# Attention in units of 32 queries and four key groups, with VectorE turning the probabilities

## The chip, the cores and the metric

The kernel runs on one core of a Trainium2 chip, in one launch. The metric is the device time of the whole program in microseconds, the median of the timed runs; lower is better. PE is TensorE's matmul stream, PEld its weight loads, DVE VectorE, ACT ScalarE, POOL GpSimd, SP the SyncE queue.

## The reference, cut to what matters

The program computes three residual layers in turn. The change touches only the first, a cross attention of 32 batches, 64 queries each, 1601 keys each, 16 heads of 16 channels; its inputs and outputs are fp32. The second layer (a cosine circuit with a small FFN) and the third (routed experts) stay as they are.

```python
# x (32, 64, 256), ctx (32, 1601, 256), H = 16, HD = 16, SCALE = 4.0
q = split_heads(layernorm(x) @ Wq.T + bq)
k = split_heads(ctx @ Wk.T + bk)
v = split_heads(ctx @ Wv.T + bv)
score = einsum('bhqd,bhkd->bhqk', q, k) * SCALE
attn = softmax(score, axis=-1)
x = x + merge(einsum('bhqk,bhkd->bhqd', attn, v)) @ Wp.T + bp
```

## The kernel before

Everything that the change touches is in `attention_and_circuit`, a raw program for each engine with semaphores; there is no scheduler, the order of every engine is written out in its own function `batches`.

One batch `n` has eight pairs of heads `p`, and each pair has one 128-row tile of scores: partition 64*e + t is head 2p+e, query t, and the 1601 keys run along the free dimension. `g = 8n + p` counts the pairs of all batches. A pair goes through these stages:

- `scores` (L952): four matmuls of 402 keys into the four banks of `ps_s`. The operands are fp32r and three parts are stacked on 96 rows (`k_st` holds high, low, high of the keys; `bd` holds high, high, low of the queries, block-diagonal over the two heads), so that one pass gives fp32 quality. `k_st` and `bd` are put together by DMAs: `stack_keys` on SP issues 48 copies of keys a batch (L246), `fill_queries` six of queries.
- `take_scores` (DVE, L636) moves all 1608 columns to `probs` in one instruction, times -4, and takes the minimum of each row into `nmax`.
- `exponentials` (ACT, L459) is one activation over 1601 columns with the row sums in `esum`.
- `turn` (PE, L963) transposes the probabilities in 13 pieces of 128x128 into the two banks of `ps_t`; ACT copies the first twelve out (`copy_tiles`, L453, three copies of 512 columns), DVE the thirteenth (`copy_tail`, L668).
- After four pairs `weigh` (L983) multiplies with the values: 13 key tiles times 4 pairs, each on 32 columns of the array, into `ps_o`. The sums of the rows are inverted, spread, turned on PE (`turn_scale`, L970) and multiplied in by `normalise` (L687 to L690). Every two batches `project_out` (L990) and `residual` make a tile of the first layer's output.

Between these, PE computes the keys and values of the next batch in 15 steps: eight of kind "k" (6 matmuls of 402 columns, from `c_hi`, `c_lo` and `w_hi`, `w_lo`), seven of kind "v" (12 matmuls of 256 columns, the last one 6). The helper `three` has the lines L915 to L917. The table `SLOT_STEPS` says which steps stand with which pair. DVE brings the keys out twice, as high and low part (L654, L656), and copies the values (L661, L663). POOL splits the context of the batch after that into high and low part (`split_ctx`, L355 to L360), from a buffer `raw` that SP fills.

The start of the program normalises x, projects the queries, stores their high and low part to DRAM (`q_scr`), and computes batch 0's keys and values before the first scores. The end of the last batch runs over into the second layer, whose orders are the tables `DVE_ORDER`, `ACT_ORDER`, `PE_ORDER`, `POOL_ORDER`.

## Time and profile before

| | us |
|---|---|
| median of 3 runs | 1943.64 (1942.24 to 1943.75) |
| span of the profiled execution | 1941.7 |
| PE busy | 1876.6 (97%) |
| PEld busy | 1777.8 (92%) |
| DVE busy | 1468.1 (76%) |
| ACT busy | 1136.1 (59%) |
| POOL busy | 652.9 (34%) |

The page gives a span and no other time for the profiled execution; it lies 1.9 us under the median of the timed runs, which also hold what stands around the first and the last instruction. Busy time is the union of the instructions of an engine. A PE instruction's duration contains the way through the array, so PE's throughput is read from the distance between starts. One fp32 matmul of the program is two PE instructions in the trace (the 52 of a `weigh` are 104); an fp32r matmul and an fp32 transpose are one.

### The profile page before, as it was taken

To read this page: it belongs to the slowest core of one execution; us is meant where nothing else is said; L and a number is where in the kernel's file an instruction comes from. 1 tells how busy PE (TensorE), PEld (TensorE's weight loads), DVE (VectorE), ACT (ScalarE), POOL (GpSimd) and SP (SyncE) were. 2 spreads that over 40 slices of the span, in tenths; PEclk is the share of its full clock that TensorE was granted. 3 is DMA by queue.
4 is the path that set the end of the run, shared out by engine and by line. 5 is a ranking of instruction groups with operands and counts; after the bars stand their busy time and mean duration, and the time that the engine had idled before them with its cause. 6 is when DMAs were issued, how large, how long until landed. Compare 5 with 4: busy or idle time off the path is not lost. (4 is left out here: it accounts for less than half of the span.)

```text
span 1941.7 us, 46658 instructions
## 1 busy us (share of the span) xinstructions
PE 1876.6 (97%) x18832; PEld 1777.8 (92%) x18832; DVE 1468.1 (76%) x2796; ACT 1136.1 (59%) x1921; POOL 652.9 (34%) x643
## 2 busy tenths in 40 slices
PE   7899999999999999999999999999879889999998
PEld 5899999999999999999999999999867789999998
DVE  6777778777777777777777778777788567766667
ACT  2465666666566656666665566656765436665552
POOL 3222223322222323222223232223031126888860
PEclk9899999999999999999999999999989799999999
DMA  8666666666666666666666666667510236666633
GB/s 272 170 155 162 156 174 169 164 157 159 161 153 167 170 167 167 157 158 157 159 167 164 170 165 162 156 163 189 149 60 23 76 118 209 225 220 218 229 115 132
DMA packets 146790, 313.85 MB, mean 162 GB/s; under 512 B 57888, under 2 KB 77216, under 8 KB 143120
## 3 DMA queue, kind: packets, MB, share of 16 engines
q1 hardware_dynamic: 140672, 295.03, 56.2%
q0 software_dynamic: 4752, 13.38, 2.3%
q8 instruction: 149, 2.44, 0.5%
q10 hardware_dynamic: 1152, 2.47, 0.5%
q14 instruction: 65, 0.53, 0.1%
HBM read 134.20 MB, written 18.35 MB: 79 GB/s over the span
## 5 line engine op out<-in xcount | busy, mean ns | idle before, releaser
L453 ACT COPY a_pT<-a_pst 128x512 f32<-128x512 f32 x768 | 421.2, 583 | 409.0 <-PE a_pst L963 409.0
L459 ACT ACTIVATE a_probs<-a_probs,a_nmax 128x1601 f32<-128x1601 f32 x256 | 418.8, 1636 | 140.0 <-DVE a_probs L636 139.8
L636 DVE TENSOR_SCALAR_CACHE_REDUCE a_probs<-a_pss 128x1608 f32<-128x1608 f32 x256 | 467.3, 1825 | 12.8 <-PE a_pss L952 12.3
L963 PE MATMUL a_pst<-a_id,a_probs 128*128 128x128 f32 (+1 forms) x3328 | 452.6, 275 | 13.7 <-ACT a_pT L453 11.5
L963 PEld LDWEIGHTS a_pst<-a_id,a_probs 128*128 128x128 f32 (+1 forms) x3328 | 382.8, 141 | 51.1 <-issue 21.0
L355 POOL TENSOR_TENSOR a_tick<-a_tick 128x1 f32<-128x1 f32 x62 | 12.0, 193 | 953.4 <-DMA a_raw<-in_ctxT 892.1
L654 DVE TENSOR_SCALAR a_khi<-a_psk,a_bk 128x402 fp32r<-128x402 f32 x250 | 158.5, 634 | 142.9 <-PE a_psk L917 141.3
L360 POOL TENSOR_TENSOR a_clo<-a_raw,a_chi 128x402 fp32r<-128x402 f32 x240 | 247.0, 1060 | 4.8
L952 PE MATMUL a_pss<-a_kst,a_bd 96*128 96x402 f32 x1024 | 240.7, 357 | 6.4 <-DVE a_v L661 5.6
L915 PE MATMUL a_pso<-a_whi,a_chi 128*128 128x256 f32 (+1 forms) x806 | 241.9, 300 | 0.0
L917 PE MATMUL a_pso<-a_whi,a_clo 128*128 128x256 f32 (+1 forms) x806 | 227.2, 282 | 0.0
L916 PE MATMUL a_pso<-a_wlo,a_chi 128*128 128x256 f32 (+1 forms) x806 | 227.1, 282 | 0.0
L952 PEld LDWEIGHTS a_pss<-a_kst,a_bd 96*128 96x128 f32 x1024 | 184.3, 190 | 20.0 <-issue 12.5
L983 PE MATMUL a_pso<-a_pT,a_v 128*32 128x128 f32 x6656 | 196.9, 275 | 0.0
L1657 PE MATMUL e_psg<-e_xh,e_guh 128*128 128x256 f32 x660 | 189.7, 287 | 5.3 <-DVE e_hl L1403 3.8
L915 PE MATMUL a_psk<-a_chi,a_whi 128*128 128x402 f32 x500 | 194.2, 388 | 0.0
L983 PEld LDWEIGHTS a_pso<-a_pT,a_v 128*32 128x32 f32 x6656 | 179.4, 111 | 12.8 <-issue 12.5
L1658 PE MATMUL e_psg<-e_xl,e_guh 128*128 128x256 f32 x660 | 186.8, 283 | 0.0
L1659 PE MATMUL e_psg<-e_xh,e_gul 128*128 128x256 f32 x660 | 186.6, 283 | 0.0
L916 PE MATMUL a_psk<-a_clo,a_whi 128*128 128x402 f32 x500 | 173.4, 347 | 0.0
L917 PE MATMUL a_psk<-a_chi,a_wlo 128*128 128x402 f32 x500 | 173.3, 347 | 0.0
L656 DVE SCALAR_TENSOR_TENSOR a_klo<-a_psk,a_bk,a_khi 128x402 fp32r<-128x402 f32 x250 | 159.0, 636 | 9.0
(251 smaller groups left out, 3511.7 us busy)
## 6 DMA issues: line engine op xcount, KB each, us to landing
a_kst<-a_khi SPq DMA_DIRECT2D x1008, 100.5 KB, 2.6
a_kst<-a_klo SPq DMA_DIRECT2D x504, 100.5 KB, 2.6
a_raw<-in_ctxT SPq DMA_DIRECT2D x60, 804.0 KB, 5.5
f_gur<-in_wgu SPq DMA_DIRECT2D x24, 1408.0 KB, 6.2
f_dr<-in_wd SPq DMA_DIRECT2D x24, 768.0 KB, 7.2
a_bd<-q_scr SPq DMA_DIRECT2D x192, 32.0 KB, 2.0
e_big<-ys_scr SPq DMA_DIRECT2D x8, 512.0 KB, 6.7
a_pT<-in_ctxT SPq DMA_DIRECT2D x2, 1608.0 KB, 9.3
```

Of the source, the lines that this page charges most:

```text
L360: last = nc.gpsimd.tensor_tensor(out=c_lo[:, s, k, cols], in0=src[:, cols], in1=c_hi[:, s, k, cols].bitcast(F32), op=ALU.subtract)
L453: nc.scalar.copy(pT[:, p % HALF, 4 * i:4 * i + 4, :], ps_t[:, i % 2, :].rearrange("p (t q) -> p t q", q=P)).then_inc(t_copied_act, 1)
L459: nc.scalar.activation(pr, pr, ACT.Exp, bias=nmax[:, b, p:p + 1], scale=-1.0, accum_out=esum[:, b, p:p + 1]).then_inc(probs_ready, 1)
L636: nc.vector.tensor_scalar(probs[:, p % 2, :].rearrange("p (b k) -> p b k", b=QK), ps_s[:, :, 0:KQ], -SCALE, None, ALU.mult, ALU.min, accum ...
L915: nc.tensor.matmul(out, a[0], b[0], start=start, stop=False)
L916: nc.tensor.matmul(out, a[0], b[1], start=False, stop=False)
L917: return nc.tensor.matmul(out, a[1], b[0], start=False, stop=stop)
L952: mm = nc.tensor.matmul(ps_s[:, q, 0:KQ], bd[:, b, p, :], k_st[:, p, q * KQ:(q + 1) * KQ], start=True, stop=True)
L963: mm = nc.tensor.transpose(ps_t[0:r, i % 2, (t % 4) * P:(t % 4 + 1) * P], probs[:, p % 2, t * P:t * P + r], a_id_sb[:])
L983: mm = nc.tensor.matmul(ps_o[32 * j:32 * j + 32, 0:P], v_sb[0:r, b, t, 32 * p:32 * p + 32], pT[0:r, j, t, :], start=(t == 0), stop=(t == K ...
L1657: nc.tensor.matmul(out, a[0], b[0], start=start, stop=False)
L1658: nc.tensor.matmul(out, a[0], b[1], start=False, stop=False)
```

## The change

The attention is cut into other units. A half `h = 2n + m` is one batch and one group `m` of eight heads. It has four units `(e, r)`: `e` is the head within each pair, `r` which 32 of the 64 queries. The keys are four groups of 400, each with the last key appended (`KG` = 401), stored in 13 tiles of 128 in which each group has 32 rows, 1664 columns in all instead of 1608. A unit's scores have partition 32*g + query (g is the key group), and the four banks of `ps_s` hold the four pairs `j`.

- `scores` is now 16 fp32 matmuls with 32 rows and 32 columns of the array each, 401 columns long, straight from `keys` (fp32, one copy) and `q_own` (the queries with the other head's channels set to zero by POOL). The stacks `k_st` and `bd`, their DMAs and the detour of the queries through `q_scr` are gone. The keys come out of PSUM once, on ACT (L484), the values too (L491); DVE copies neither.
- `take_scores` is four instructions of 401 columns, `exponentials` four activations of 401 columns.
- The minimum of a row must be shared by the four key groups, since they are one softmax: for every two units PE turns `nmax` (`turn_max`), DVE takes the minimum over groups (`reduce_max`), PE spreads it (`spread_max`), ACT copies it (`copy_bias`).
- `turn` is one VectorE transpose of 1664 columns in blocks of 32x32, from `probs` (a ring of 5) to `pT` (6 slots). The transposes on PE and the copies out of `ps_t` are gone.
- `weigh` has 52 matmuls a half as before, with the four units' columns as its moving operand. The sums of the rows go through POOL (`less_extra` takes the three surplus copies of the last key out, `spread_sums`) and four small matmuls; `normalise` divides.
- The steps have 416 columns for keys; the last value tile has 128 rows.

PE in the middle of the loop before: a key step, one pair's scores, and the transposes of the pair before (a_khi, a_psk, a_kst are key tiles, a_pst the turned probabilities).

```order
L963 MATMUL a_pst<-a_id,a_probs 65x128
L915 MATMUL a_psk<-a_chi,a_whi 128x402
L916 MATMUL a_psk<-a_clo,a_whi 128x402
L917 MATMUL a_psk<-a_chi,a_wlo 128x402
L915 MATMUL a_psk<-a_chi,a_whi 128x402
L916 MATMUL a_psk<-a_clo,a_whi 128x402
L917 MATMUL a_psk<-a_chi,a_wlo 128x402
L952 MATMUL a_pss<-a_kst,a_bd 128x402 x4
L963 MATMUL a_pst<-a_id,a_probs 128x128 x8
```

PE at the turn of a half in the changed kernel: the end of a value step, the spread minima, the weighting, the sums, and the next unit's scores.

```order
L879 MATMUL a_psk<-a_whi,a_chi 128x256
L880 MATMUL a_psk<-a_wlo,a_chi 128x256
L881 MATMUL a_psk<-a_whi,a_clo 128x256
L934 MATMUL a_psm<-a_id,a_low 32x8 x4
L953 MATMUL a_pso<-a_pT,a_v1 32x128 x52
L957 MATMUL a_pso<-a_sin,a_marks 32x128 x4
L919 MATMUL a_pss<-a_keys,a_qown 32x401 x16
L879 MATMUL a_psl<-a_chi,a_whi 128x416
L880 MATMUL a_psl<-a_clo,a_whi 128x416
```

So the 13 transposes with each pair have left PE, and a unit's scores are 16 small matmuls where a pair's were four. DVE before, one pair and the beginning of the next:

```order
L636 TENSOR_SCALAR a_probs,a_nmax<-a_pss 128x1608
L661 COPY a_v<-a_pso 128x512
L668 COPY a_pT<-a_pst 65x128
L654 TENSOR_SCALAR a_khi<-a_psk,a_bk 128x402
L656 SCALAR_TENSOR_TENSOR a_klo<-a_psk,a_bk,a_khi 128x402
```

and DVE in the changed kernel, from the fourth unit of one half to the second of the next:

```order
L662 TENSOR_SCALAR a_probs,a_nmax<-a_pss 128x401 x4
L677 STREAM_TRANSPOSE a_pT<-a_probs 128x1664
L668 TENSOR_REDUCE a_low<-a_psm 8x32
L662 TENSOR_SCALAR a_probs,a_nmax<-a_pss 128x401 x4
L677 STREAM_TRANSPOSE a_pT<-a_probs 128x1664
L687 RECIPROCAL a_sT<-a_pso 128x128
L691 SCALAR_TENSOR_TENSOR a_op<-a_pso,a_marks,a_sT 128x64 x2
L695 SCALAR_TENSOR_TENSOR a_oT<-a_op,a_bv 128x64
L662 TENSOR_SCALAR a_probs,a_nmax<-a_pss 128x401 x4
```

The three copies from PSUM with each pair have left DVE and one transpose with each unit has come.

The diff, cut to its core:

```diff
         def _(dve):
+            def take_scores(h, i):
...
+                for j in range(HALF):
+                    at_max = HALF * (i % 2) + j
+                    nc.vector.tensor_scalar(probs[:, at % RING, j, 0:KG], ps_s[:, j, 0:KG], -SCALE, None,
+                                            ALU.mult, ALU.min, accum_out=nmax[:, group % 2, at_max:at_max + 1]).then_inc(max_ready, 1)
...
+            def turn(h, i):
...
+                nc.vector.transpose(pT[:, turned_slot(h, i)].rearrange("p j k -> p (j k)"), probs[:, at % RING].rearrange("p j k -> p (j k)")).then_inc(turned, 1)
...
+            def period(h):
+                for i in range(HALF):
+                    if h + 1 < NH:
+                        take_scores(h + 1, i)
+                    if i == 1 and h % 4 == 0 and h > 0:
+                        residual(h // 4 - 1)
+                    if h >= 0:
+                        turn(h, i)
+                    if i == 0 and h > 0:
+                        normalise(h - 1)
+                    if i % 2 == 1 and h + 1 < NH:
+                        reduce_max(2 * (h + 1) + i // 2)
...
         def _(pe):
-                for q in range(QK):
-                    mm = nc.tensor.matmul(ps_s[:, q, 0:KQ], bd[:, b, p, :], k_st[:, p, q * KQ:(q + 1) * KQ], start=True, stop=True)
+                for g in range(QK):
+                    for j in range(HALF):
+                        mm = nc.tensor.matmul(ps_s[32 * g:32 * g + 32, j, 0:KG], q_own[32 * j:32 * j + 32, n % 2, m, e, 32 * r:32 * r + 32],
+                                              keys[32 * j:32 * j + 32, m, g * KG:(g + 1) * KG], start=True, stop=True)
...
+            def period(h):
+                steps = steps_in(h)
+                if h > 0:
+                    weigh(h - 1)
+                if h + 1 < NH:
+                    scores(h + 1, 1)
+                for z in steps[0]:
+                    step(*z)
...
+                if h + 1 < NH:
+                    turn_max(2 * h + 2)
+                    scores(h + 1, 2)
+                for z in steps[1]:
+                    step(*z)
+                if h + 1 < NH:
+                    spread_max(2 * h + 2)
+                    scores(h + 1, 3)
+                for z in steps[2]:
+                    step(*z)
+                if h + 1 < NH:
+                    turn_max(2 * h + 3)
+                if h + 2 < NH:
+                    scores(h + 2, 0)
+                for z in steps[3]:
+                    step(*z)
+                if h + 1 < NH:
+                    spread_max(2 * h + 3)
```

`scores` waits until DVE has taken all four banks of the unit before (`max_ready`), and `take_scores` waits for the scores (`s_filled`). `normalise(h-1)` stands on DVE between the first and the second unit of a period and waits for `weigh(h-1)`, which PE runs at the start of that period. `turn(h, i)` waits for that unit's exponentials, which ACT makes between the copies of the steps' results.

## Rows read from the trace of the kernel before

**Rows 1.** The page's busy times, and a stretch of the loop (busy us, clock).

```profile
PE 1876.6 (97%) x18832; PEld 1777.8 (92%) x18832; DVE 1468.1 (76%) x2796; ACT 1136.1 (59%) x1921; POOL 652.9 (34%) x643
...
600.00:1000.00 400.00, 399.43 (x4368) 381.14 (x4367) 314.68 (x564) 245.83 (x375) 109.69 (x114) 1.00 0.65 163
```

**Rows 2.** The waits: who waited for whom, us, times, longest.

```profile
ACT a_pT L453 <- PE a_pst L963: 409.0, 317, 3.2
DVE a_khi L654 <- PE a_psk L917: 141.3, 186, 0.8
```

**Rows 3.** Timeline of PE (start us, us): first line of one `weigh`, two batches earlier.

```profile
616.67 3.05 PE L983 MATMUL a_pso<-a_pT,a_v 128*32 128x128 f32 x104
```

**Rows 4.** Timeline of all engines around the `weigh` at 702.56.

```profile
700.82 1.83 DVE L636 TENSOR_SCALAR_CACHE_REDUCE a_probs<-a_pss 128x1608 f32<-128x1608 f32 x1
...
702.36 0.27 PE L970 MATMUL a_pst<-a_id,a_sc 128*128 128x128 f32 x1
...
702.56 2.78 PEld L983 LDWEIGHTS a_pso<-a_pT,a_v 128*32 128x32 f32 x104 [0.17 <-issue]
702.56 3.05 PE L983 MATMUL a_pso<-a_pT,a_v 128*32 128x128 f32 x104
702.57 0.09 DVE L636 DVE_READ_ACCUMULATOR a_probs<-a_pss 128x1 f32 x1
...
702.93 1.64 ACT L459 ACTIVATE a_probs<-a_probs,a_nmax 128x1601 f32<-128x1601 f32 x1
...
704.47 0.19 ACT L459 ACTIVATION_READ_ACCUMULATOR a_probs<-a_probs,a_nmax 128x1 f32 x1
...
705.54 1.01 PE L952 MATMUL a_pss<-a_kst,a_bd 96*128 96x402 f32 x4
705.75 0.23 DVE L687 TENSOR_TENSOR a_os<-a_pso,a_sT 128x64 f32<-128x64 f32 x1 [1.49 <-PE a_pso L983]
705.89 0.22 DVE L688 TENSOR_TENSOR a_pso<-a_pso,a_sT 128x64 f32<-128x64 f32 x1
```

**Rows 5.** Timeline of PE: a value step from 707.18 to 708.68.

```profile
707.18 0.36 PE L915 MATMUL a_pso<-a_whi,a_chi 128*128 128x256 f32 x1
...
708.68 0.71 PE L963 MATMUL a_pst<-a_id,a_probs 128*128 128x128 f32 x5
```

**Rows 6.** Timeline of PE: key step, scores, eight transposes, next value step.

```profile
709.15 0.43 PE L915 MATMUL a_psk<-a_chi,a_whi 128*128 128x402 f32 x1
...
710.33 0.91 PE L952 MATMUL a_pss<-a_kst,a_bd 96*128 96x402 f32 x4
711.08 1.04 PE L963 MATMUL a_pst<-a_id,a_probs 128*128 128x128 f32 x8
711.87 0.36 PE L915 MATMUL a_pso<-a_whi,a_chi 128*128 128x256 f32 x1
```

**Rows 7.** Instructions of single lines: ns minimum/median/maximum, first and last start us.

```profile
L915 PE MATMUL a_psk<-a_chi,a_whi x500: 339/387/748, 30.9 to 1385.5; 128*128 128x402 f32 x167
...
L983 PE MATMUL a_pso<-a_pT,a_v x6656: 269/273/423, 80.1 to 1434.1; 128*32 128x128 f32 x180, 65*32 65x128 f32 x16
...
L680 DVE TENSOR_TENSOR a_sc<-a_rinv,a_own x64: 291/294/2237, 77.9 to 1425.5; 128x128 f32<-128x128 f32 x64
```

**Rows 8.** Groups by line and shape: xcount, busy us, mean ns, idle before.

```profile
L1151 PE MATMUL f_psf<-f_w,f_hT 128*128 128x256 f32 x256 | 58.4, 388 | 0.8 <-ACT f_hT L616 0.8
...
L661 DVE COPY a_v<-a_pso 128x512 f32<-128x512 f32 x186 | 128.6, 691 | 43.1 <-PE a_pso L917 42.9
...
L741 DVE TENSOR_SCALAR f_t<-f_u 128x512 f32<-128x512 f32 x8 | 3.3, 417 | 0.0
...
L864 DVE TENSOR_TENSOR_SCAN f_t<-f_c,f_hd 128x512 f32<-128x512 f32 x4 | 4.9, 1217 | 0.0
...
L459 ACT ACTIVATE a_probs<-a_probs,a_nmax 128x1601 f32<-128x1601 f32 x256 | 418.8, 1636 | 140.0 <-DVE a_probs L636 139.8
...
L616 ACT ACTIVATE f_hT<-f_psh,f_b 128x512 f32<-128x512 f32 x16 | 10.2, 684 | 7.9 <-PE f_psh L1141 7.7
...
L360 POOL TENSOR_TENSOR a_clo<-a_raw,a_chi 128x402 fp32r<-128x402 f32 x240 | 247.0, 1060 | 4.8
```

More of the change, by code:

```diff
@@ new lines, in _ @@
+            for h in range(NH - 2):
+                period(h)
+            sp.wait_ge(kv_filled, STEPS * B)
+            for dst, src in ((row[:], rows), (id_sb[:], ident), (b1_sb[:], b1), (w2_sb[:], w2), (wr_sb[:], wr), (rb_sb[:], rb)):
+                sp.dma_start(dst, src).then_inc(loaded, 16)
+            sp.wait_ge(x1_free, 16 * (NT - 1) + 1)
+            sp.dma_start(x_t[:], x[NT - 1]).then_inc(x_loaded, 16)
+            sp.dma_start(x1[:, NT - 2, :], x1_scr[NT - 2]).then_inc(x1_loaded[group_of[-1]], 16)
@@ L546, in _ @@
+            for h in range(-1, NH):
+                period(h)
             act.wait_ge(expo_set, 1)
@@ L814, in _ @@
+            for h in range(-1, NH):
+                period(h)
             ch = Chain(dve, dv)
@@ new lines, in turn_max, with spread_max @@
+            def turn_max(group):
+                pe.wait_ge(max_ready, 2 * HALF * (group + 1))
+                if group > 0:
+                    pe.wait_ge(bias_ready, group)
+                nc.tensor.transpose(ps_m[0:2 * HALF, 0:P], nmax[:, group % 2, :], a_id_sb[:]).then_inc(max_turned, 1)
+            def spread_max(group):
+                pe.wait_ge(max_reduced, group + 1)
+                for g in range(QK):
+                    mm = nc.tensor.matmul(ps_m[32 * g:32 * g + 32, P:P + 2 * HALF], lowest[:, group % 2, :], a_id_sb[0:2 * HALF, 0:2 * HALF], start=True, stop=True)
+                mm.then_inc(max_spread, 1)
@@ L1097, in _, with period @@
[L1097 to L1098 removed]
+            pe.wait_ge(cleared, 3)
+            for s in range(FIRST_STEPS):
+                step(0, s)
+            scores(0, 0)
+            def period(h):
+                steps = steps_in(h)
+                if h > 0:
+                    weigh(h - 1)
[3 more added lines that the diff above has]
+                    step(*z)
+                    if h % 4 == 0 and h > 0 and z == steps[0][0]:
+                        project_out(h // 4 - 1)
+                if h % 4 == 0 and h > 0 and not steps[0]:
+                    project_out(h // 4 - 1)
+                if h % 4 == 0 and h > 0:
+                    pe.wait_ge(x1_ready, h // 4)
+                if h + 1 < NH:
[8 more added lines that the diff above has]
+                    step(*z)
+                if h + 1 < NH:
+                    turn_max(2 * h + 3)
[3 more added lines that the diff above has]
+                    step(*z)
+                if h + 1 < NH:
+                    spread_max(2 * h + 3)
@@ L1099, in idle_work @@
+            for h in range(-1, NH):
+                period(h)
             def idle_work(n):
```

762 lines of the change are left out of this document (315 added, 447 removed), and 6 rows, old and new, of tables (ACT_ORDER, DVE_ORDER, PE_ORDER).

## The prediction

> **What bounds the kernel now.** I read the busy times first: PE is busy for 1876.6 of 1941.7 us, and in a stretch of 400 us of the loop for 399.43, at a granted clock of 1.00 (2.4 GHz) [rows 1]. Then the waits: ACT waits 409.0 us for PE's transposes and DVE 141.3 us for PE's key steps [rows 2], while PE waits for nobody. So the loop is as long as PE's stream. One `weigh` starts at 616.67 [rows 3] and the same one two batches on at 702.56 [rows 4]: 42.95 us a batch. The steps begin at 30.9 and the last `weigh` begins its last matmuls at 1434.1 [rows 7]: the stretch that the change touches is 1403 us, the other 539 us stay.
>
> PE's parts are read from start to start. Key step 709.15 to 710.33 = 1.18 us; scores of a pair 710.33 to 711.08 = 0.75; eight transposes 711.08 to 711.87 = 0.79 [rows 6]. Value step 707.18 to 708.68 = 1.50 and five transposes 708.68 to 709.15 = 0.47 [rows 5, 6]. `weigh` with its way in and out 702.36 to 705.54 = 3.18 with one small transpose in it, so about 3.1 [rows 4]. A batch: 8 x (0.75 + 0.79 + 0.47) = 16.1, keys 9.4, values 6 x 1.50 + 0.75 = 9.75, weights 6.2, small things 0.6: 42.1 of the 42.95.
>
> **The change on PE.** It removes the 16.1. Kept: key steps of 416 instead of 402 columns, 8 x 1.22 = 9.8; values 9.8; weights 6.2; output projection 0.25. Added: the sums, eight small instructions each half, 2 x 0.25 = 0.5; `turn_max` and `spread_max`, 4 x 0.24 = 1.0. Without scores this is 27.5 us.
>
> The scores are the term that decides. A unit has 16 fp32 matmuls, 32 instructions in the trace. How long does one occupy its tile? 128 columns last 273 ns [rows 7], 256 columns 388 [rows 8], so 0.90 ns a column: 401 columns take 0.36 us and two instructions one after the other 0.71. No row shows tiles of 32 rows. If all 16 run at once, a unit takes 0.71 plus staggering; if only the four column tiles overlap, 8 x 0.36 = 2.9; if nothing does, 32 x 0.36 = 11.5. The nearest row is `weigh`: 104 instructions of 128 columns in 2.98 us (702.56 to 705.54) are 28.7 ns each, where one alone takes some 0.11, so four column tiles do run at once in fp32, each with its own moving stream from all partitions [rows 4]. The new tiling reads no more streams from a partition than that; new is that four row tiles write into four banks at the same partitions. I take 0.80 and keep 2.9 as the upper end (11.5 would need even the overlap of `weigh` to be lost). 8 x 0.80 = 6.4.
>
> Changing the size of the tiles costs something: before `weigh` PEld is idle 0.17 us by "issue" [rows 4], and the way in and out of `weigh` was about 0.3 us more than its stream. A batch has 8 units of scores, entered and left, and 8 small maxima and spreads: 24 changes by 0.17 = 4.1 us; the bounds are 0 (hidden under the end of the work before) and 24 x 0.25 = 6.0.
>
> The Trainium skill, TensorEngine Tiling (Array Packing), "Key Properties", says that a change of the tiling mode drains the engine; the 0.17 us of [rows 4] agrees in kind. TensorE: Matmul & The Clock Gate, Part 3, reports a packing of 4x4 tiles at 10.6 times the speed of single matmuls; by that, 32 x 0.36 / 10.6 = 1.09 us a unit would be an estimate, 2.3 us a batch over my term. No row here shows it.
>
> PE: 27.5 + 6.4 + 4.1 = **38.0 us a batch**.
>
> **DVE.** It loses the key and value copies and gains the transposes. Taking: 1608 columns last 1.83 us, but the next instruction and the accumulator's read both start 1.75 after the start [rows 4]. The 1207 columns fewer at 1.04 ns (1.83 against 691 ns for 512 columns [rows 4, 8]) leave 0.50 for 401 columns; with the accumulator's 0.09 read apart and no overlap 0.57 + 0.09 = 0.66. I take 0.55, since the read overlapped in the row, with a little for four in a row: 2.2 a unit. Transpose of 1664 columns: no row shows one. Bounds from one-input and scan instructions: 512 columns SBUF to SBUF at 417 ns (about 0.52 ns a column, 1.0 us) and a scan at 1217 ns (about 2.1 a column, 3.6 us) [rows 8]; the taking's rate of 1.04 gives 1.87. I take 1.85, the middle rate, at which most instructions of this engine run. Sum: 8 x (2.2 + 1.85) = 32.4; four `reduce_max` at 0.28 and two `normalise` at about 1.0 (as two of 0.23 and 0.22 and their dependents [rows 4]), the residual's half: 3.8. **36.2 us**.
>
> VectorE (DVE) Microarchitecture Reference, section 3.8, of the Trainium skill says that the transpose front end sustains one element per cycle and lane; by that page it is the middle rate too, and no row here shows it.
>
> **ACT.** It loses three copies of 512 columns a pair, gains the key and value copies, and has four short exponentials for one long. 1601 columns last 1.64 and the accumulator's read starts at 1.54 [rows 4]; against 684 ns at 512 columns [rows 8] that is 0.87 ns a column, so 401 last about 0.59; with the read 0.19 apart 0.78, overlapped as in the row 0.6. I take 0.65: 32 x 0.65 = 20.8, fifteen copies at 0.5 = 7.5, maxima 0.7: **29 us**. POOL keeps its split (8 x 1.06 [rows 8] and the casts) and adds about 16 tiny instructions and two spreads of 512 columns, some 20 us of 38. The 48 + 6 DMAs a batch go; they were beside the path (PE waited for none in the loop) and give nothing.
>
> **How they fit together.** PE 38.0, DVE 36.2, ACT 29: no engine has room to hide another's latency, and they are in lock step. Walk one half, PE's share 19.0. A unit of scores needs the taking of the unit before; the taking needs the scores (0.17 after the last start) and comes after the transpose (1.85). PE has after the scores (0.80 + 0.34) two steps (2.72), 3.9 in all; DVE has 4.05 + 0.28 every second unit. So in the three units without `weigh` DVE is slightly the slower one, and PE waits some tenths before `turn_max` and the scores; in the fourth, `weigh` puts PE 3.4 us ahead of DVE's need, and DVE waits for it at `normalise`, since it only has one taking and one transpose (4.05) before it while PE comes late by up to a step (2.7 + 3.4). Adding the durations along this chain gives 0.6 us of PE waiting a half. **39.3 us a batch.**
>
> The whole: four first steps and a unit, 6; the period that fills the pipe, 21; 62 halves with steps at 19.65, 1218; one half with no steps, bound by DVE (4 x 4.05 + 0.6), 17; the last transposes 9; the last weighting 3.4: 1274, and some 5 less since the last halves overlap. 1270 against 1403 is -133. From the profiled span 1941.7 that is 1808.7, and with the 1.9 that the median lies above it **1811 us**.
>
> **The rivals.**
> 1. *Dearer small instructions.* DVE and ACT at their upper bounds (0.66; 0.78), and transposes held up by POOL: L680, a DVE instruction between two SBUF tensors, has a median of 294 ns and a maximum of 2237 [rows 7]. DVE 8 x (2.64 + 1.95) + 3.8 = 40.5, with waits 42. +2.7 x 31 = +84: 1895.
> 2. *Half the overlap of row tiles*, 1.4 us a unit: +4.8 a batch, less the waits that PE's lateness removes, 42.8 to 43: +3.7 x 31 = +115: 1926. For: no row has it. Against: separate banks.
> 3. *The other side: the DVE transpose at half rate*, 3.6 us. DVE becomes the bound: 8 x (2.2 + 3.6) + 3.8 = 50.2, nothing else late. +10.9 x 31 = +338: 2149. It decides from where DVE's batch passes 43.6, that is a transpose of 2.8 us. For: the data must be filled and drained, in fp32; the scan shows that this engine has instructions at such a rate. Against: most do not.
> 4. *Row tiles do not overlap*, 2.9 us a unit: 54.8 a batch, +15.5 x 31 = +480: 2291.
> 5. *PE's clock falls* to 1.2 GHz in the waits. The stretch of [rows 1] had 1.00 throughout with PE never idle; the new waits are tenths of a microsecond. All of PE's 38 us at half clock would be 76 a batch, a quarter of the loop so would add 300.
>
> **How the numbers follow.** My forecast 0.63, rival 1 0.10, rival 2 0.07, rival 3 0.09, rival 4 0.08, rival 5 0.03. The forecast's own range, with changes of tile size at 0.05 to 0.25 us and takings at 0.50 to 0.60, is 36.8 to 41 us a batch: 1735 to 1865. The range of 8 in 10 takes in rivals 1 and 2: 1735 to 1960. Faster: 0.63 + 0.09 of rival 1 + 0.03 of rival 2 = 0.75. Same (within 0.2%, 4 us, about what a measurement of this kernel can tell): 0.03, from 1 and 2. Slower 0.22.
>
> **What would show it.** In the profile of the changed kernel: a unit's 32 instructions of L919 in about 0.8 us from start to the next step's start (step 1 of the forecast; 1.4 or 2.9 for rivals 2 and 4); L677 at about 1.9 us (3.6 for rival 3); L662 starts 0.55 apart; L465 starts 0.65 apart; successive first lines of L953 19.65 us apart; PE over 90% busy at a clock of 1.00, DVE over 90%. A DVE near 100% with PE waiting for L662 by whole microseconds, or a clock under 1.00 in the loop, would make the prediction wrong; so would a PE busy all the time with scores longer than 1.4 us.

## The result, and the profile after

The changed kernel takes **1827.74 us** (median of 4 runs, 1826.5 to 1828.59) where the kernel before, in runs beside it, took 1942.94 (1941.53 to 1943.75): a ratio of 0.941, 95% interval 0.939 to 0.942. The prediction was 1811 with a range of 1735 to 1960. The profiled execution has a span of 1824.6 us, against the 1808.7 of the sum.

The page's busy times and the same stretch of the loop as in [rows 1]; the columns of the second line are the stretch, PE, PEld, DVE, ACT and POOL busy, the granted clock, the DMA share and GB/s:

```profile
PE 1652.9 (91%) x24272; PEld 1360.0 (75%) x24272; DVE 1566.3 (86%) x3585; ACT 1199.9 (66%) x3297; POOL 892.4 (49%) x1283
```

```profile
600.00:1000.00 400.00, 367.39 (x6607) 284.05 (x6605) 377.12 (x879) 289.13 (x854) 191.82 (x328) 1.00 0.15 48
```

PE was busy for 399.43 of these 400 us and is now for 367.39; DVE was at 314.68 and is now, at 377.12, the busier one. Neither is full. The clock is 1.00 (2.4 GHz) as before. The DMAs' share fell from 0.65 to 0.15; PE had waited for none of them in the loop.

Who waits for whom in 600 to 1000 (us, times, longest), in the place of [rows 2]:

```profile
PEld a_psm L928 <- DVE a_probs L662: 34.3, 36, 1.2
...
PE a_psm L928 <- DVE a_probs L662: 27.0, 36, 1.0
...
DVE a_sT L687 <- PE a_pso L953: 16.0, 10, 1.6
...
PE a_pss L919 <- DVE a_probs L662: 3.0, 5, 0.6
```

(L662 is `take_scores`, here called a taking; L928 is `turn_max`.) The waits have turned round: PE now waits for DVE's takings, ahead of `turn_max`, and DVE for PE's `weigh`. The lines of the loop that cost DVE and PE most (busy us, mean ns of one, idle before):

```profile
L662 DVE TENSOR_SCALAR_CACHE_REDUCE a_probs<-a_pss 128x401 f32<-128x401 f32 x328 | 169.1, 572 | 3.3 <-DVE a_pT L677 3.3
L677 DVE STREAM_TRANSPOSE a_pT<-a_probs 128x1664 f32<-128x1664 f32 x82 | 156.1, 1904 | 0.0
...
L919 PE MATMUL a_pss<-a_keys,a_qown 32*32 32x401 f32 x2592 | 78.1, 507 | 3.0 <-DVE a_probs L662 3.0
...
L687 DVE RECIPROCAL a_sT<-a_pso 128x128 f32<-128x128 f32 x20 | 19.2, 958 | 17.8 <-PE a_pso L953 16.0 <-issue 1.8
L695 DVE SCALAR_TENSOR_TENSOR a_oT<-a_op,a_bv 128x64 f32<-128x64 f32 x20 | 17.8, 892 | 0.7
```

The timeline where one `weigh` ends, a unit of scores runs and the normalisation follows (start us, us; compare [rows 4]):

```profile
607.55 0.40 PE L957 MATMUL a_pso<-a_sin,a_marks 128*32 128x128 f32 x8
...
607.88 0.97 PE L919 MATMUL a_pss<-a_keys,a_qown 32*32 32x401 f32 x32
608.08 0.96 DVE L687 RECIPROCAL a_sT<-a_pso 128x128 f32<-128x128 f32 x1 [0.18 <-issue]
...
608.29 3.12 POOL L313 TENSOR_TENSOR a_clo<-a_raw,a_chi 128x416 fp32r<-128x416 f32 x3
...
608.79 0.46 PE L879 MATMUL a_psk<-a_chi,a_whi 128*128 128x416 f32 x1
...
609.07 0.48 DVE L691 SCALAR_TENSOR_TENSOR a_op<-a_pso,a_marks,a_sT 128x64 f32<-128x64 f32 x2
...
609.58 0.89 DVE L695 SCALAR_TENSOR_TENSOR a_oT<-a_op,a_bv 128x64 f32<-128x64 f32 x1
...
610.39 0.56 DVE L662 TENSOR_SCALAR_CACHE_REDUCE a_probs<-a_pss 128x401 f32<-128x401 f32 x1
```

A unit's 32 instructions hold PE for 0.90 us (607.88 to 608.79). The normalisation holds DVE for 2.31 us (608.08 to 610.39), while POOL subtracts beside it; the taking of the unit whose scores were ready at about 608.9 has to wait for that. The first instructions of successive `weigh` alternate at 18.5 and 20 to 21.4 us; two batches are 78.4 us, **39.2 a batch** against 42.95.

### The profile page after: what moved, and what is told of

Same layout as the page of the kernel before. It is cut to its first block and busy times, and to the rows that moved or that the text cites. A ratio compares the mean times of both kernels' runs of the same rounds, so it can differ in the third digit from the quotient of the medians.

```text
span 1824.6 us, 59184 instructions
## 1 busy us (share of the span) xinstructions
PE 1652.9 (91%) x24272; PEld 1360.0 (75%) x24272; DVE 1566.3 (86%) x3585; ACT 1199.9 (66%) x3297; POOL 892.4 (49%) x1283
## 3 DMA queue, kind: packets, MB, share of 16 engines
q1 hardware_dynamic: 38416, 130.71, 21.4%
## 5 line engine op out<-in xcount | busy, mean ns | idle before, releaser
L465 ACT ACTIVATE a_probs<-a_probs,a_bias 128x401 f32<-128x401 f32 x1024 | 632.2, 625 | 0.0
L662 DVE TENSOR_SCALAR_CACHE_REDUCE a_probs<-a_pss 128x401 f32<-128x401 f32 x1024 | 527.8, 572 | 25.5 <-PE a_pss L919 14.9
L677 DVE STREAM_TRANSPOSE a_pT<-a_probs 128x1664 f32<-128x1664 f32 x256 | 487.3, 1904 | 0.0
L919 PE MATMUL a_pss<-a_keys,a_qown 32*32 32x401 f32 x8192 | 248.0, 509 | 14.2 <-DVE a_probs L662 13.5
L313 POOL TENSOR_TENSOR a_clo<-a_raw,a_chi 128x416 fp32r<-128x416 f32 x240 | 250.2, 1074 | 0.0
L465 ACT ACTIVATION_READ_ACCUMULATOR a_probs<-a_probs,a_bias 128x1 f32 x1024 | 197.2, 193 | 0.0
L484 ACT ACTIVATE a_keys<-a_psk,a_bk 128x401 f32<-128x401 f32 x131 | 77.4, 591 | 96.9 <-PE a_psk L881 96.9
L484 ACT ACTIVATE a_keys<-a_psl,a_bk 128x401 f32<-128x401 f32 x125 | 73.9, 592 | 95.2 <-PE a_psl L881 95.2
L1592 PEld LDWEIGHTS e_psg<-e_xh,e_guh 128*128 128x128 f32 x660 | 125.6, 190 | 6.4 <-issue 6.4
L1593 PEld LDWEIGHTS e_psg<-e_xl,e_guh 128*128 128x128 f32 x660 | 125.7, 191 | 0.0
L1594 PEld LDWEIGHTS e_psg<-e_xh,e_gul 128*128 128x128 f32 x660 | 125.6, 190 | 0.0
L879 PE MATMUL a_psl<-a_whi,a_chi 128*128 128x256 f32 x428 | 123.6, 289 | 0.0
L491 ACT COPY a_v<-a_psl 128x512 f32<-128x512 f32 x99 | 58.0, 586 | 94.9 <-PE a_psl L881 94.9
```

What stands on the lines that cost most here:

```text
L313: last = nc.gpsimd.tensor_tensor(out=c_lo[:, n % 2, k, cols], in0=src[:, cols], in1=c_hi[:, n % 2, k, cols].bitcast(F32), op=ALU.subtract)
L465: nc.scalar.activation(z, z, ACT.Exp, bias=bias[:, group % 4, at_bias:at_bias + 1], scale=-1.0, accum_out=esum[:, h % 2, j, 2 * e + r:2 * ...
L484: nc.scalar.activation(keys[:, m, q * KG:(q + 1) * KG], step_bank(at)[:, 0:KG], ACT.Identity, bias=bk_sb[:, m:m + 1]).then_inc(kv_copied, 1)
L662: nc.vector.tensor_scalar(probs[:, at % RING, j, 0:KG], ps_s[:, j, 0:KG], -SCALE, None, ALU.mult, ALU.min, accum_out=nmax[:, group % 2, at ...
L677: nc.vector.transpose(pT[:, turned_slot(h, i)].rearrange("p j k -> p (j k)"), probs[:, at % RING].rearrange("p j k -> p (j k)")).then_inc( ...
L879: nc.tensor.matmul(out, a[0], b[0], start=start, stop=False)
```

## The experiments

All kernels are edits of the changed kernel, and their times are put beside its 1827.7 us; the ratios are to the kernel before, in runs beside each.

### 1. A unit's scores twice

```diff
-                for g in range(QK):
+                for g in 2 * tuple(range(QK)):
```

> The changed kernel with every unit of scores issued twice into the same banks (the result is the same): TensorE gets 16 more small matmuls, 32 instructions, in each of 248 units, and nothing else changes. A unit's two bursts of 16 start 0.36 us apart, so the second unit adds 0.72 us, 8 x 0.72 = 5.8 us a batch. Theory A (lock step: TensorE 36 and VectorE 37 of 39.2 us a batch, each waiting for the other at handovers): nearly all of it shows, +4.5 to +5.8 a batch over 31 batches, so +140 to +180: 1970 to 2010 us, slower than the kernel before. Rival B (VectorE alone sets the loop, TensorE has its 3.2 us a batch of idle time to give): +2.6 a batch, +80: 1908. Rival C (TensorE's stream alone sets it): +5.8, +180: 2008.

Measured: 1970.1 us, ratio 1.014 (1.012 to 1.016), 43.4 us a batch, +4.2. Timeline of PE, a doubled unit and the step behind it:

```profile
601.30 1.98 PE L919 MATMUL a_pss<-a_keys,a_qown 32*32 32x401 f32 x64
603.21 0.46 PE L879 MATMUL a_psk<-a_chi,a_whi 128*128 128x416 f32 x1
```

The pair of units takes 1.91 us, so the second one costs 1.01 and not 0.72: of its 64 instructions the first 32 start in bursts 6.7 ns apart, the later ones 16.7 ns. TensorE got 8.1 us more a batch. Its waits of 3.2 us took up a part of that, and it is now busy for 399.13 of 400 us: 36.0 + 8.1 would be 44.1, the batch is 43.4. The time is the one that A named, but not for A's reason, since only half of the added work shows; with the real price of 8.1, B's reasoning (the waits absorb it first) gives +4.9. So this run doesn't tell A from B; it shows how much TensorE could still take. Experiment 3 tells them apart.

### 2. A full-size matmul in the middle of each unit

```diff
                                               keys[32 * j:32 * j + 32, m, g * KG:(g + 1) * KG], start=True, stop=True)
+                    if g == 1:
+                        nc.tensor.matmul(ps_s[:, 0, 480:488], a_id_sb[:], a_id_sb[:, 0:8], start=True, stop=True)
```

> The changed kernel with one full-size fp32 matmul of 8 columns (two short instructions, into unused columns of the scores' bank) set into the middle of every unit of 32x32 tiles: two more changes of tile size a unit, 16 a batch, 496 in all. The step of the forecast that is tested is 0.17 us a change. Theory A: the trace shows some 0.17 us of extra spacing at each change, 0.35 to 0.45 a unit with the two short instructions; 16 x 0.2 = 3.2 us a batch if TensorE's time shows in full, +80 to +110: 1910 to 1935 us. Rival: changes are hidden under the end of the work before, 0.05 each: +0.8 a batch, 1830 to 1850. Rival: a change costs 0.3 and more, since the pipeline empties for 401 columns: over 1960.

Measured: 1986.3 us, ratio 1.023 (1.021 to 1.025): outside all three expectations. Timeline of PE, one broken unit:

```profile
604.21 0.86 PE L919 MATMUL a_pss<-a_keys,a_qown 32*32 32x401 f32 x11
604.99 0.39 PE L922 MATMUL a_pss<-a_id 128*128 128x8 f32 x2
605.31 0.90 PE L919 MATMUL a_pss<-a_keys,a_qown 32*32 32x401 f32 x16
606.14 0.46 PE L879 MATMUL a_psk<-a_chi,a_whi 128*128 128x416 f32 x1
```

The break itself is cheap: 0.32 us from 604.99 to 605.31 for two short instructions and the change back. What I had left out is that half a unit, 16 instructions, takes 0.83 us (605.31 to 606.14) where all 32 take 0.90. A unit is two instructions of 401 columns one after the other and the way out, however many tiles run beside each other; the second eight matmuls cost 0.07. The price of a break is that of a second, half-filled unit.

The price of a change can be read in these rows. From the last instructions of 401 columns to the next step are 0.43 us; where such instructions follow one another on the same tiles they are 0.34 apart (experiment 4). That is 0.09 us, not the 0.17 of the forecast, and from `spread_max` to the scores there is none (0.03 us between their first starts, 604.13 and 604.16 in this run).

### 3. Half of VectorE's transposes

```diff
-                nc.vector.transpose(pT[:, turned_slot(h, i)].rearrange("p j k -> p (j k)"), probs[:, at % RING].rearrange("p j k -> p (j k)")).then_inc(turned, 1)
+                nc.vector.transpose(pT[:, turned_slot(h, i), 0:2].rearrange("p j k -> p (j k)"), probs[:, at % RING, 0:2].rearrange("p j k -> p (j k)")).then_inc(turned, 1)
...
-                        moving = pT[:, first:first + 4, j, cols]
+                        moving = pT[:, first:first + 4, j % 2, cols]
```

> The changed kernel where VectorE turns only the first two of a unit's four pairs (832 of 1664 columns), and the weighting reads those two for all four: half of the transposes is left out, and the output is that of two pairs used twice. VectorE loses 0.87 to 0.92 us in each of 8 units a batch, 7 us; TensorE's instructions stay the same in number and size. Theory A (lock step, TensorE's own stream 36 to 37 us a batch): the loop falls to 37 to 37.7 and then waits for TensorE alone, -1.5 to -2.2 a batch: 1758 to 1782 us. Rival B (VectorE alone sets the loop): -6 to -7 a batch, 1610 to 1640. Rival C (TensorE's stream sets it already): no change, 1825.

Measured: 1786.7 us, ratio 0.919 (0.918 to 0.921), 38.0 us a batch, between A and C. The stretch 600 to 1000, DVE's transposes in it, and the waits:

```profile
600.00:1000.00 400.00, 377.94 (x6773) 294.02 (x6772) 318.99 (x905) 295.12 (x875) 196.76 (x335) 1.00 0.16 51
```

```profile
L677 DVE STREAM_TRANSPOSE a_pT<-a_probs 128x832 f32<-128x832 f32 x84 | 87.2, 1038 | 0.0
```

```profile
DVE a_sT L687 <- PE a_pso L953: 50.0, 21, 3.0
...
PE a_psm L928 <- DVE a_probs L662: 15.2, 16, 1.1
```

Seven us of VectorE's 37 a batch are gone and the batch is only 1.2 shorter: VectorE's throughput is not the bound, and rival B is out. PE still waits before `turn_max`: four takings last 2.0 us from the scores on, however free the engine is, and where the normalisation stands before them it is 2.3 us more. What is left of PE's idle time, 2.1 us a batch, is such handovers.

### 4 to 6. Tiles of 128 rows, and the order inside a unit

```diff
-                        mm = nc.tensor.matmul(ps_s[32 * g:32 * g + 32, j, 0:KG], q_own[32 * j:32 * j + 32, n % 2, m, e, 32 * r:32 * r + 32],
-                                              keys[32 * j:32 * j + 32, m, g * KG:(g + 1) * KG], start=True, stop=True)
+                        mm = nc.tensor.matmul(ps_s[32 * g:32 * g + 32, j, 0:KG], q_own[:, n % 2, m, e, 32 * r:32 * r + 32],
+                                              keys[:, m, g * KG:(g + 1) * KG], start=True, stop=True)
```

> The changed kernel with the scores in tiles of all 128 rows by 32 columns in place of 32 by 32: the same 16 matmuls and 32 instructions a unit into the same places, but the four pairs of one column tile now follow one another (each sums over all pairs' dimensions, so the scores are other numbers). It gives the price of the rival in which row tiles don't overlap. Forecast of that rival: a unit takes 4 x 0.72 = 2.9 us in place of 0.72 to 0.9. TensorE gets +2.0 to 2.1 a unit, +16.5 a batch; less its 3 us of idle time: 52.5 to 55 a batch, 2240 to 2320 us. If a unit stays under 1.4 us here, the gain is from the column tiles alone, and the overlap of row tiles is worth little: 1830 to 1950.

> The changed kernel with a unit's 16 matmuls in another order: pair by pair, and in it the four key groups, in place of group by group, and in it the four pairs. Same tiles, same sizes, same result. Theory A (all 16 tiles of 32x32 run at once, each with its own row and column tile): the order is of no account, 0.90 us a unit, 1824 to 1831 us. Rival: tiles that follow one another in a column tile overlap worse than tiles of different column tiles (the run in which the tiles had all 128 rows took 6.94 us a unit in the first order, where four full-speed column tiles give 2.9): then this order is shorter, 0.8 a unit, -0.8 a batch, 1800 to 1810, or the other way round longer.

> The kernel whose scores go in tiles of 128 rows by 32 columns (each sums over all pairs, other numbers) in the order pair by pair, so that four matmuls in a row go to four different column tiles; group by group it took 6.94 us a unit. Theory (an instruction waits at the head of TensorE's queue until its own column tile is free, and nothing behind it may pass): now the four column tiles run side by side, 8 rounds of 0.34 us = 2.8 to 3.0 us a unit, +2.1 over the changed kernel, 52 to 55 us a batch, 2220 to 2330 us. Rival (column tiles don't overlap in fp32 at 401 columns at all): 32 x 0.34 = 11 us a unit, or 6.9 as before: 3200 us or more.

In 5 and 6 the loop over the pairs stands outside and that over the key groups inside:

```diff
-                for g in range(QK):
-                    for j in range(HALF):
+                for j in range(HALF):
+                    for g in range(QK):
```

Measured, with the length of a unit from its first start to the next step's:

| scores in | order | unit us | batch us | time us |
|---|---|---|---|---|
| 32x32 tiles | group by group (the changed kernel) | 0.90 | 39.2 | 1827.7 |
| 32x32 tiles | pair by pair (5) | 0.90 | 39.2 | 1828.4 (ratio 0.941, 0.940 to 0.943) |
| 128x32 tiles | group by group (4) | 6.94 | 83.5 | 3248.4 (ratio 1.672) |
| 128x32 tiles | pair by pair (6, one run) | 2.81 | 50.7 | 2197.2 |

Timeline of PE in experiment 4, one unit:

```profile
600.94 7.01 PE L919 MATMUL a_pss<-a_keys,a_qown 128*32 128x401 f32 x32
607.88 0.46 PE L879 MATMUL a_psk<-a_chi,a_whi 128*128 128x416 f32 x1
```

Experiment 4 was far off my 2.9 us. Single instructions in it start 0.337 us apart, and in most of the unit only two column tiles are at work: the four matmuls of one column tile stand in a row, each waits for the one before, and those behind, for free column tiles, wait with them. Experiment 6 sends four in a row to four column tiles: four start within 0.02 us, the next four 0.337 later, eight rounds. That bears out the theory given for it. It is also the price of rival 4: 2.81 us a unit as forecast (2.9), but 2197 us and not 2291. What is left of the batch beside the scores is 28.2 us (50.7 - 8 x 2.81) where the forecast had 31.6, which is 105 us of the time, and the end is 16 us longer than forecast. In 32x32 tiles all 16 run at once, so the order is of no account. The row tiles alone are worth 1.9 us a unit, 370 us of the time (one run of 6): without them the change would have been a loss.

### 7. A shorter way through the normalisation

```diff
-                nc.vector.reciprocal(scale_T[:], ps_o[:, P:2 * P]).then_inc(sum_inverse, 1)
+                nc.vector.reciprocal(scale_T[:, 0:SQ], ps_o[:, P:P + SQ]).then_inc(sum_inverse, 1)
...
-                    nc.vector.scalar_tensor_tensor(out=o_part[:, e, :], in0=ps_o[:, cols], scalar=mark[:, e:e + 1], in1=scale_T[:, cols],
+                    nc.vector.scalar_tensor_tensor(out=ps_o[:, 2 * P:2 * P + SQ] if e else o_part[:, 0, :], in0=ps_o[:, cols], scalar=mark[:, e:e + 1], in1=scale_T[:, 0:SQ],
...
-                nc.vector.scalar_tensor_tensor(out=oT[:, m, SQ * b:SQ * (b + 1)], in0=o_part[:, 0, :], scalar=bv_sb[:, m:m + 1],
-                                               in1=o_part[:, 1, :], op0=ALU.add, op1=ALU.add).then_inc(o_normed, 1)
+                nc.vector.scalar_tensor_tensor(out=oT[:, m, SQ * b:SQ * (b + 1)], in0=ps_o[:, 2 * P:2 * P + SQ], scalar=bv_sb[:, m:m + 1],
+                                               in1=o_part[:, 0, :], op0=ALU.add, op1=ALU.add).then_inc(o_normed, 1)
...
-                    mm = nc.tensor.matmul(ps_o[32 * j:32 * j + 32, P:2 * P], mark[:, ONES], sums_in[:, j].rearrange("p q b -> p (q b)"), start=True, stop=True)
+                    for e in range(2):
+                        mm = nc.tensor.matmul(ps_o[32 * j:32 * j + 32, P:P + SQ], of_head[:, e].rearrange("p a b -> p (a b)"),
+                                              sums_in[:, j, 2 * e:2 * e + 2].rearrange("p q b -> p (q b)"), start=(e == 0), stop=(e == 1))
```

`of_head` holds ones in the columns of head 0 or 1 of a pair and zeros elsewhere.

> The changed kernel with a shorter way through the normalisation on VectorE, same result: TensorE's eight small matmuls put only each row's own head's sum into 64 columns (in place of both heads' in 128), so the reciprocal has 64 columns in place of 128 (957 ns now, about 0.48 if it goes by columns), and the second of the two products goes to PSUM, so that the last instruction has one input in SBUF in place of two and isn't held up beside GpSimd's subtraction (844 ns in the mean now, 284 where GpSimd was quiet). VectorE loses 0.48 + 0.56 = 1.0 us a half, 2.1 a batch. Theory A (lock step; leaving out 7 us of VectorE's batch gave only 1.2): -0.8 to -1.2 a batch, since the time falls where TensorE waits for the taking after it: 1790 to 1803 us. Rival B: half of it or less, since the waits move elsewhere: 1805 to 1820. Rival C (VectorE alone): -2.1 a batch, 1762.

Measured: 1785.9 us, ratio 0.920 (0.918 to 0.921), 37.8 us a batch: -42, a little more than the upper end of A. DVE's lines in 600 to 1000:

```profile
L692 DVE RECIPROCAL a_sT<-a_pso 128x64 f32<-128x64 f32 x21 | 11.7, 558 | 20.6 <-PE a_pso L958 18.3 <-issue 2.4
...
L706 DVE TENSOR_TENSOR a_x<-a_x,a_bp 128x256 f32<-128x256 f32 x5 | 6.7, 1338 | 0.0
...
L700 DVE SCALAR_TENSOR_TENSOR a_oT<-a_pso,a_bv,a_op 128x64 f32<-128x64 f32 x21 | 6.0, 284 | 0.8
```

The last product is back at 284 ns and the reciprocal at 558 (0.40 less, not 0.48). VectorE lost 1.0 us a half and the loop gained 0.7 of it; the 7 us a batch of experiment 3 gained no more (1786.7 us). What counts is where the work stands: between a unit's scores and its takings. How much of the gain is the reciprocal's and how much the last product's was not taken apart. But the hold-up has moved on, to the residual's addition, 1338 ns where it was 416. The timeline shows what it is beside:

```profile
664.73 4.18 POOL L315 TENSOR_TENSOR a_clo<-a_raw,a_chi 128x416 fp32r<-128x416 f32 x4
...
667.85 1.33 DVE L706 TENSOR_TENSOR a_x<-a_x,a_bp 128x256 f32<-128x256 f32 x1
...
669.69 0.27 PE L933 MATMUL a_psm<-a_id,a_nmax 128*8 128x128 f32 x1 [0.71 <-DVE a_x L709]
```

### 8. Keeping TensorE at work where the steps have ended

```diff
+            def keep_busy(n):
+                for _ in range(n):
+                    nc.tensor.matmul(ps_k0[:, 0:D], a_id_sb[:], wp_sb[:, 0, :], start=True, stop=True)
...
+                if h == NH - 1:
+                    keep_busy(36)
...
+                    if h == NH - 2:
+                        keep_busy(10)
```

> The changed kernel with TensorE kept at work in the last two periods of the loop, where it has no more steps: ten matmuls of 256 columns (2.3 us) behind each unit's scores and 36 (8.4 us) behind the next to last weighting, into a free bank that nobody reads; nothing else changes. In the changed kernel the granted clock is 0.73 in 1270:1290, 0.59 in 1290:1310 and 0.74 in 1310:1330, and the last two weightings' streams take 5.0 and 5.5 us in place of 2.9. Theory A (the lower clock costs there): the clock stays at 0.95 or more, both weightings at 2.9 us, -4 to -5 us at the end: 1820 to 1824 us. Rival (VectorE's transposes set the end and only the very last weighting counts): -2.5, 1825. Rival (the filling gets in the way of the maxima or the last weighting): +1 to +4.

Measured: 1835.9 us, ratio 0.945 (0.943 to 0.947), 8 us longer and outside all three expectations. A filling matmul takes 0.44 us, twice what I had put, so the maxima and the next to last `weigh` came late (it started at 1296.6, not 1288.4). It is repeated with less filling in experiment 11.

### 9. The residual's bias on GpSimd

```diff
                 less_extra(h, 0)
+                if h % 4 == 0 and h > 0:
+                    pool.wait_ge(x_loaded, 16 * (h // 4))
+                    pool.wait_ge(const_loaded, 16 * CONSTS)
+                    nc.gpsimd.tensor_tensor(out=x_t[:], in0=x_t[:], in1=bp_sb[:], op=ALU.add).then_inc(x1_biased, 1)
...
-                nc.vector.tensor_tensor(x_t[:], x_t[:], bp_sb[:], ALU.add).then_inc(x1_biased, 1)
+                if t == NT - 1:
+                    nc.vector.tensor_tensor(x_t[:], x_t[:], bp_sb[:], ALU.add).then_inc(x1_biased, 1)
```

> The kernel with the shorter normalisation (1785.9 us), in which the bias of the residual (one addition of 256 columns every fourth half, two inputs in SBUF) goes from VectorE to GpSimd, ahead of its cast; same result. In the shorter kernel this addition took 1338 ns (416 before, in the changed kernel): the hold-up beside GpSimd's subtraction had moved from the normalisation to it, and the batches with a residual last 38.95 us where the others last 36.6. Theory A (it is that hold-up, on the way TensorE waits for): those batches lose about 1.2 us, 0.6 a batch in the mean, 16 in all, -15 to -20: 1766 to 1771 us. Rival B (the longer batches come from TensorE's output projection and from waiting for PSUM, not from the hold-up): -0 to -5, 1781 to 1786. Rival C (the addition on GpSimd delays its cast and the sums): slower than 1786.

Measured: **1766.6 us**, ratio 0.909 (0.908 to 0.911), the shortest of all. The batches with a residual fell from 38.95 to 37.6 to 37.9 us, the others stay at 36.6. PE is at 385.42 of 400 (first the stretch, then the addition on GpSimd with its minimum, median and maximum in ns):

```profile
600.00:1000.00 400.00, 385.42 (x7106) 304.16 (x7099) 374.80 (x925) 300.83 (x896) 207.12 (x351) 1.00 0.17 53
```

```profile
L375 POOL TENSOR_TENSOR a_x<-a_x,a_bp x15: 731/732/742, 132.2 to 1173.6; 128x256 f32<-128x256 f32 x15
```

GpSimd needs 732 ns for what VectorE did in 416, and had them to spare.

### 10 to 12. The end of the loop

```diff
-        TURNS_IN = {0: (0,), 1: (1,), 2: (2,), 3: (3, 4, 5, 6)}
+        TURNS_IN = {0: (), 1: (), 2: (), 3: (0, 1, 2, 3, 4, 5, 6)}
```

This is the edit of 10. 11 is experiment 8 with 5 and 20 filling matmuls in place of 10 and 36; 12 has the edits of 7, 9 and 10 together, and the filling with 5 and 15.

> The changed kernel with the six rounding instructions (three pairs, 1.1 us each) of the next stage that stand between VectorE's last four transposes put behind the last of them; same work, same result. Theory A (they stand in front of the last weighting, which starts at 1304.4): it starts 2.2 to 3.3 us earlier, and the end of the kernel follows by part of it, since VectorE's list behind it is the same length: -1 to -3, 1825 to 1827. Rival (the last weighting isn't what the end waits for, VectorE's list is): 1828, no change.

> The changed kernel with TensorE kept at work in the last two periods by fewer matmuls: a filling matmul of 256 columns took 0.44 us in the trace, twice what I had put, so that ten behind a unit delayed the maxima (the last but one weighting started at 1296.6 in place of 1288.4, but its stream took 2.9 us at a clock of 1.00 in place of 5.0). Now five behind each unit (2.2 us, where TensorE is free for 3) and 20 (8.9 us) behind the last but one weighting (free for 12). Theory A (the lower clock costs time there): both weightings at 2.9 us, the clock above 0.9 until 1310, -3 to -5: 1823 to 1825 us. Rival (what the clock costs is given back, since VectorE's list sets the end): 1827 to 1829.

> All of it in one kernel, same result: the shorter normalisation, the residual's bias on GpSimd, the rounding instructions behind the last transpose, and TensorE kept at work in the last two periods (five matmuls a unit and 15 behind the last but one weighting). Theory A (the parts add up): 1786 - 17 - 2 - 3 = 1764 us, 1758 to 1770. Rival (the end of the loop is bound by VectorE's list, so that only the loop's gain counts): 1769 to 1772. Rival (GpSimd's addition is in the way): 1786 and more.

Measured, and what the traces show of the last `weigh` and of VectorE's first scan (L828 in the changed kernel), with which the second layer begins:

| kernel | time us | last `weigh` starts | its last start | first scan | end minus first scan |
|---|---|---|---|---|---|
| before | 1942.9 | - | 1434.1 | 1428.3 | 513.4 |
| changed | 1827.7 | 1304.4 | 1309.8 | 1312.5 | 512.2 |
| 10, rounding late | 1827.3 | 1300.0 | 1305.1 | 1311.2 | 512.5 |
| 11, TensorE kept at work | 1829.9 | 1306.0 | 1308.8 | 1314.1 | 513.7 |
| 9 | 1766.6 | 1241.3 | 1246.6 | 1249.4 | 514.9 |
| 12, all of it | 1767.6 | 1238.4 | 1241.1 | 1249.6 | 516.7 |

The last two `weigh` in the changed kernel and in 11 (timeline of PE):

```profile
1288.39 5.14 PE L953 MATMUL a_pso<-a_pT,a_v 128*32 128x128 f32 x104
...
1304.41 5.65 PE L953 MATMUL a_pso<-a_pT,a_v 128*32 128x128 f32 x104 [10.66 <-DVE a_pT L677]
```

```profile
1291.20 3.04 PE L953 MATMUL a_pso<-a_pT,a_v 128*32 128x128 f32 x104
...
1305.99 3.05 PE L953 MATMUL a_pso<-a_pT,a_v 128*32 128x128 f32 x104 [2.69 <-DVE a_pT L677]
```

The stretches around them, first the changed kernel, then 11:

```profile
1270.00:1290.00 20.00, 9.70 (x266) 5.97 (x270) 19.71 (x45) 18.31 (x58) 7.12 (x16) 0.73 0.32 101
1290.00:1310.00 20.00, 9.34 (x199) 8.47 (x192) 15.85 (x20) 11.15 (x28) 10.06 (x16) 0.59 0.01 1
```

```profile
1280.00:1300.00 20.00, 17.20 (x217) 13.74 (x216) 15.55 (x31) 17.57 (x52) 6.73 (x16) 1.00 0.04 12
```

In 1290 to 1310 of the changed kernel TensorE was busy for 9.34 of 20 us and the mean clock was 0.59, so most of that stretch ran at 1.2 GHz, and a `weigh` took 5.1 to 5.7 us. Kept at work TensorE had 2.4 GHz until 1300, and both took 3.05.

The last `weigh` is not what the end waits for. It is over 4.7 us earlier in 10 than in the changed kernel, and 5.5 earlier in 12 than in 9; the times differ by -0.4 and +1.0, and the runs overlap (1825.6 to 1827.8 against 1826.5 to 1828.6; 1765.7 to 1769.1 against 1766.4 to 1767.0). So the rival of 10 holds. 12 (ratio 0.909, 0.908 to 0.911) lies in the range of its theory A, but over 9 it gained nothing: only the loop's gain is there.

The last `weigh` but one is another matter. In the changed kernel VectorE waits for it, and from the reciprocal behind it VectorE works without a pause to the first scan:

```profile
1293.88 0.96 DVE L687 RECIPROCAL a_sT<-a_pso 128x128 f32<-128x128 f32 x1 [3.94 <-PE a_pso L953]
...
1308.65 2.58 DVE L737 TENSOR_SCALAR f_t<-f_u 128x512 f32<-128x512 f32 x1
```

| kernel | last but one `weigh`, first to last start | reciprocal behind it | to the first scan |
|---|---|---|---|
| changed | 1288.4 to 1293.3 | 1293.9 | 18.6 |
| 10 | 1287.6 to 1292.1 | 1292.7 | 18.5 |
| 11 | 1291.2 to 1294.0 | 1294.6 | 19.5 |
| 9 | 1225.3 to 1230.1 | 1230.8 | 18.6 |
| 12 | 1228.1 to 1230.8 | 1231.5 | 18.1 |

From the first scan to the end there are 512 to 517 us in all six kernels. So the chain of the end is this `weigh`, VectorE's list of 18 to 19 us, and the rest, and the lower clock does cost time on it: 2.1 us of the changed kernel (5.14 against 3.04 us). Experiment 11 took these 2.1 us back and lost more: its filling ahead of the `weigh` had it start 2.8 us later, and two instructions of VectorE's list took 0.9 us more, so that its 1829.9 us (1829.4 to 1833.3) lie above both of its expectations. That the time did not fall shows that this filling does not pay, and not that the fallen clock is free; a filling that leaves the maxima and this start alone was not tried.

## Why the prediction was right, and where its steps were off

The direction and the loop came out as forecast: 39.2 us a batch against 39.3. Two errors of about 2 us in it cancel: TensorE's own work came out 2.0 us a batch lower than forecast, its waits 2.0 higher. That the mechanism (TensorE and VectorE in lock step, 16 tiles at once) was right is shown by experiments 3, 4 and 6; that the number of the loop was right to 0.1 us is luck.

- **TensorE**: forecast 38.0 us a batch, measured 36.0 (367.39 / 400 x 39.2). The step on the scores held: 16 tiles at once, 0.90 us a unit against 0.80, which is +0.8 a batch. The mis-sized term is the 24 changes of tile size at 0.17: 0.09 or nothing each (experiment 2). What the other terms leave for them is some 1.9 in place of 4.1; this sum is worked out, not measured. The 0.17 of [rows 4] was PEld's idle time; a good part of it lay beside matmuls still running, so it does not show an engine that stands empty, and the distance of PE's own starts should have been used. The key steps are 1.15 us, not 1.22.
- **VectorE**: forecast 36.2, measured 37.0. Takings start 0.50 apart (0.55 forecast), the transpose takes 1.83 from start to start (1.85): a unit is 3.82, not 4.05. The term that failed is `normalise`: "two at about 1.0" was carried over from the products of before, and it takes 2.31. The reciprocal of 128 columns is 958 ns, which no row of before had at that size, and the last product, between two SBUF inputs beside POOL's subtraction, 892 in place of 284. I had [rows 7] in hand, where L680 goes up to 2237 ns, and put that risk on the transposes (rival 1), which have one input and show none (1877 to 1908 ns); it fell on the last product, which has two. One input is no safeguard in general: L737 of the second layer, one input of 512 columns from SBUF, took 2.58 us beside a subtraction on POOL (L443, 1308.26 to 1310.95) where it took 0.38 at 1304.28.
- **Waits**: forecast 0.6 us a half, measured 1.6 (400 - 367.39 us in 400, 3.2 a batch). That is this same 1.3 us of `normalise` ahead of the takings: experiments 7 and 9, which take it off, bring the wait down to 1.3 us a batch and the time by 61 us.
- **The end**: the sum was 16 us too low, and all of it lies here. The loop up to the last `weigh` but two was 5 us ahead of the forecast. The mis-sized terms are "the last transposes 9 ... and some 5 less" and the 539 us that I kept fixed behind the last weighting. From the last `weigh` but one to the last there are 16.0 us (1288.4 to 1304.4): that `weigh` at the lower clock, the normalisation, three transposes and three pairs of VectorE's rounding instructions for the next layer. The last matmuls start at 1309.8, 9.2 us behind the 1300.6 of the sum, and stand 7.3 us further from the end than before. In the kernel before, the rounding instructions lay in VectorE's waits for PE, and the first scan was 6 us ahead of the last matmuls; in the changed one three pairs stand between the last transposes and four behind them, where VectorE waits for nobody, and the first scan comes 2.7 us behind. The right mark was the first scan, which has moved by 115.8 us of the 117.1 between the two spans.

The rivals. 1 (dearer small instructions): takings and exponentials (0.615 apart) are at the lower end, its hold-up exists but elsewhere. 2 and 4 (row tiles): 0.90 us a unit, and experiment 6 shows what they would have cost. 3 (half-rate transposes): 1904 ns for 1664 columns, 1038 for 832, 1.04 ns a column, the rate of the takings before. What the Trainium skill, Vector Engine (DVE) Microarchitecture Reference, section 3.8, says of the transpose (one element per cycle and lane) agrees with that. 5 (the clock): 1.00 in the loop, down at its end, where it costs some 2 us. The Trainium skill, TensorE: Matmul & The Clock Gate, Part 3, has 10.6 times the speed for 4x4 tiles, by which the estimate was 1.09 us a unit. This case measured 0.90, so the packing is worth some 12 times here (32 x 0.337 / 0.90).

Not settled: whether the rest of TensorE's idle time (1.3 us a batch in experiment 9) can be got by moving `turn_max` behind a further step. It wasn't tried. Nor is it settled how much of the 2.1 us that the lower clock costs at the end can be had back.

## What to carry to other kernels

Where two engines are each above 90% and pass work to and fro, as here, the total work of either says little; price the instructions that stand between one engine's result and the next engine's need, and take those away first: 2 us a batch there gave 42 us, 7 us elsewhere 41. Cost every instruction of a new short chain from a row of its own operation and operand places, not from its neighbours. When a loop gets shorter, look for the mark from which the rest really follows (here VectorE's first scan of the next stage, and ahead of it the `weigh` that VectorE last waits for) before you keep the rest fixed.
